# Decoder layer in one core: the FFN weights' own stage taken apart and spread over its neighbours

## What is computed

```python
x = x + attention(layernorm(x), q_w, q_b, k_w, k_b, v_w, v_b, o_w, o_b)   # causal, 16 heads of 32
x = x + long_convolution(ctx, ctx, layernorm(x), ssm_kernel, D)           # kv outer products, convolved, times q
x = x + ffn(layernorm(x), w_gate_up, w_down)

def _quant_dequant(v, axis):
    scale = jnp.max(jnp.abs(v), axis=axis, keepdims=True) / QMAX
    scale = jnp.maximum(scale, EPS)
    q = jnp.clip(jnp.round(v / scale), -QMAX, QMAX)
    return q * scale

gate, up = xq @ w1q.T             # xq: tokens quantised by row; w1q: w_gate_up (2816 x 512), by row
h = silu(gate) * up
out = hq @ w2q.T                  # hq: h quantised by row; w2q: w_down (512 x 1408), by row
```

## Time and profile before

| | |
|---|---|
| median of 3 runs (lowest, highest) | 1241.2 us (1239.53 to 1241.73) |
| the profiled execution, its own time | 1243.32 us |
| its span in the profile | 1241.5 us |
| busy: PE, DVE, POOL, ACT | 1142.1, 1006.6, 963.1, 880.2 us |
| mean granted TensorE clock | 0.965 |
| DMA moved | 186.57 MB, mean 150 GB/s |

### The profile page before, as it was taken

One profiled execution on the slowest core, in us unless ns is written; L12 is line 12 of the kernel. 1 busy time (PEld: TensorE's weight loads), 2 busy tenths in 40 slices (PEclk: granted clock), 3 DMA queues, 4 the chain that ended last, 5 costly groups with the idle time before them and its releaser, 6 DMA issues. The chain is left out here.

```text
span 1241.5 us, 33761 instructions
## 1 busy us (share of the span) xinstructions
PE 1142.1 (92%) x10142; PEld 815.6 (66%) x10142; DVE 1006.6 (81%) x3165; ACT 880.2 (71%) x1815; POOL 963.1 (78%) x1112
## 2 busy tenths in 40 slices
PE   7989999999999999998756799999999999999996
PEld 5767777777777777875435566666666666666652
DVE  4678878878788887887486798888988988988885
ACT  3678888878788887888564366766667666667665
POOL 1286887767777776787833999999999999999993
PEclk8979999999999999999775999999999999999999
DMA  6346755556555555655382444434444333444310
GB/s 206 93 154 193 235 167 171 183 173 190 178 176 171 159 185 166 189 163 182 143 287 70 128 136 142 128 109 131 137 144 140 123 112 129 142 144 132 112 62 26
DMA packets 87840, 186.57 MB, mean 150 GB/s; under 512 B 12176, under 2 KB 28816, under 8 KB 87760
## 3 DMA queue, kind: packets, MB, share of 16 engines
q1 hardware_dynamic: 86896, 185.02, 47.2%
q10 hardware_dynamic: 864, 0.66, 0.3%
HBM read 105.86 MB, written 54.61 MB: 129 GB/s over the span
## 5 line engine op out<-in xcount | busy, mean ns | idle before, releaser
L649 ACT ACTIVATE prob<-masked,negmax 128x128 f32<-128x128 f32 (+1 forms) x512 | 206.4, 454 | 67.6 <-DVE negmax L777 66.6
L777 DVE CUSTOM_DVE_ANT_0 masked<-s_ps,mask_f 128x128 f32<-128x128 f32 (+1 forms) x512 | 161.1, 352 | 34.0 <-PE s_ps L530 21.5
L1028 PE MATMUL y_ps<-kv,toep 128*128 128x288 f16 x640 | 184.2, 288 | 1.4 <-DVE prod L1390 1.4
L1029 PE MATMUL y_ps<-kv,toep 128*128 128x288 f16 x640 | 183.8, 287 | 0.0
L1030 PE MATMUL y_ps<-kv,toep 128*128 128x288 f16 x640 | 183.8, 287 | 0.0
L1086 PE MATMUL f_ps<-w1T,xiT 128*128 128x512 bf16 (+1 forms) x768 | 172.9, 361 | 0.9 <-ACT xiT L1222 0.7
L1286 POOL TENSOR_TENSOR tree<-prod 128x512 f32<-128x512 f32 x128 | 163.3, 1276 | 1.3 <-DVE prod L1390 1.3
L1229 ACT ACTIVATE silu<-gate,sx 128x512 f32<-128x512 f32 (+1 forms) x96 | 66.0, 687 | 134.4 <-DVE gate L1454 134.3
L409 POOL TENSOR_TENSOR kv_s<-kv_f,kv_s 128x1152 f16<-128x1152 f32 x64 | 152.2, 2379 | 0.6 <-ACT kv_s L663 0.6
L783 DVE TENSOR_TENSOR pT_lo<-t_ps,pT_hi 128x384 f16<-128x384 f32 x256 | 140.7, 550 | 12.2 <-ACT pT_hi L657 11.7
L657 ACT CAST pT_hi<-t_ps 128x384 f16<-128x384 f32 x256 | 122.4, 479 | 34.4 <-PE t_ps L539 33.1
(11 more groups left out here) (162 smaller groups left out, 3505.6 us busy)
## 6 DMA issues: line engine op xcount, KB each, us to landing
kv_pairs<-kv_s SPq DMA_DIRECT2D x64, 576.0 KB, 3.3
kv<-kv_pairs SPq DMA_DIRECT2D x32, 1152.0 KB, 8.1
c_in<-in_ctxr SPq DMA_DIRECT2D x64, 192.0 KB, 2.5
x_in<-in_x SPq DMA_DIRECT2D x16, 512.0 KB, 6.4
q_st<-q_hi SPq DMA_DIRECT2D x128, 64.0 KB, 2.0
k_st<-k_hi SPq DMA_DIRECT2D x128, 64.0 KB, 2.0
x_res<-in_x SPq DMA_DIRECT2D x16, 512.0 KB, 5.9
x_after_attention<-x_out SPq DMA_DIRECT2D x16, 512.0 KB, 4.3
```

Of the source, the lines that this page charges most:

```text
L649: ins = nc.scalar.activation(prob[h % 2][:, at:at + w], masked[h % 2][:, at:at + w], ACT.Exp, bias=negmax[:, h % 2, t:t + 1], scale=-1.0)
L777: ins = nc.vector.tensor_tensor_reduce(masked[h % 2][:, at:at + w], s_ps[h % 2][:, at:at + w], mask_f[:, S - w:S], -1.0, FAR, ALU.add, ALU ...
L1028: nc.tensor.matmul(dst, toep[p][:, 0, taps], c[:, 0, m], start=mt == 0, stop=False)
L1029: nc.tensor.matmul(dst, toep[p][:, 0, taps], c[:, 1, m], start=False, stop=False)
```

## The change

The weights stage is gone, and so is its wait of all engines. Its work is spread over three places:

- **Attention's last two rounds**: SP loads all 22 blocks of w_gate_up in 11 loads of 512 KB (`W.load`) and the first convolution's operands (`first_conv`). DVE finds maxima and scales, and ACT scales the rows, for units 0 to 3 between the heads of round 15 and for units 4 to 6 around JOBS_END. The stage no longer waits for `x_stored`.
- **The mixer's beginning**: SP waits for `x_stored` and loads the first tokens and w_down. DVE finds the maxima of units 7 to 10, ACT scales the rows of 7 and 8. PE turns ten half units (four f32 blocks of 128 x 128 each, L194 of the changed kernel) in place, with the rounding constant still on them, then the scales. DVE or ACT takes each set out of PSUM and subtracts the constant on the way.
- **Mixer rounds 0 and 1**: 24 more sets and the scales of w_down, 3 sets at each of five places in round 0 and 2 at each of five in round 1, the maxima of units 11 to 14 and the row scaling of units 9 to 14.

The scales go to HBM and come back as a broadcast DMA (`load_scales`) where before a product with ones spread them. w1T, w2T, q, k, the turned tokens and one convolution buffer now share memory with others. At the program's beginning, the two bias broadcasts are issued later, the key weights are split in two halves, wv is loaded ahead of the second sequence, and `weights_high(2)`, `weights_low(2)`, `row_stats(1)` and `normalise(1)` stand later in their queues.

```diff
+UNITS = [(1, n, 2) for n in range(0, 2 * 11, 2)] + [(2, n, 1) for n in range(DT)]
+N_W1 = 11
+IN_ROUND, IN_TAIL = 4, 7
+UNIT_MAX = {1: 0, 4: 1, 7: 2, 10: 3}
+UNIT_SCALE = {3: 0, 6: 1, 9: 2, 12: 3}
...
+    def home(self, u):
+
+        return self.raw[u // 2][:, u % 2 * 2:u % 2 * 2 + 2, :] if u < 8 else self.x_all[:, 2 * u - 16:2 * u - 14, :]
...
+    def target(self, u, b, nb):
+
+        w, n, _ = UNITS[u]
+        if w == 1:
+            return self.w1T[:, :, (n + b // DT) * P:(n + b // DT + 1) * P]
+        return self.w2T[:, b:b + nb, n * P:(n + 1) * P]
...
+    def find_maxima(self, dve, u):
+        dve.wait_ge(self.loaded[u], 16)
+        rows = self.rows(u)
+        self.nc.vector.tensor_reduce(self.maxima[:, self.columns(u)],
+                                     rows.rearrange("p (k d) -> p k d", d=D) if UNITS[u][0] == 1 else rows, AX_X, ALU.max,
+                                     apply_absolute_value=True).then_inc(self.max_done, 1)
...
+    def scale_rows(self, act, u):
+
+        w, _, k = UNITS[u]
+        rows, inv = self.rows(u), self.inv[:, self.columns(u)]
+        act.wait_ge(self.inv_done, u + 1)
+        for n in range(k):
+            part = rows[:, n * D:(n + 1) * D] if w == 1 else rows
+            ins = self.nc.scalar.activation(part, part, ACT.Copy, bias=MAGIC, scale=inv[:, n:n + 1])
+        ins.then_inc(self.scaled, 1)
...
+    def turn_rows(self, pe, u, b, nb, bank, eye_f):
+        pe.wait_ge(self.scaled, u + 1)
+        rows = self.rows(u)
+        for t in range(nb):
+            mm = self.nc.tensor.transpose(bank[:, t * P:(t + 1) * P], rows[:, (b + t) * P:(b + t + 1) * P], eye_f[:])
+        return mm
...
+        w1T = wqkv[:].rearrange("p a t d -> p (a t d)").bitcast(BF16)[:, 0:DT * 2 * I_FF].rearrange("p (t d) -> p t d", t=DT)
+        w2T = x_all[:].rearrange("p a d -> p (a d)").bitcast(BF16)[:, 0:IT * D].rearrange("p (t d) -> p t d", t=IT)
+        toep_0 = x_all[:, 4 * TT - 1, :].bitcast(F16).rearrange("p (a d) -> p a d", a=2)
+        toep_loaded, kv_loaded = ([top.enter_context(nc.semaphore(f"{n}{p}")) for p in range(2)] for n in ("toep_loaded", "kv_loaded"))
+        W = Weights(nc, top, w1T, w2T, x_all)
...
+    SMALLS = [(bq_raw[:], bq), (bk_s[:], bk), (mask_f[:, S - P:], mask)]
     SMALL = len(SMALLS)
+    BIASES = [(bv_b[:], bv.broadcast_to([P, D])), (bo_b[:], bo.broadcast_to([P, D]))]
+
+    W_PARTS = [[slice(0, D)], [slice(0, D // 2), slice(D // 2, D)], [slice(0, D)], [slice(0, D)]]
+    split_after = lambda n, part=-1: sum(len(W_PARTS[k]) for k in range(n)) + part % len(W_PARTS[n]) + 1
...
+            load_weights(2, wvT)
             load(1)
-            load_weights(2, wvT)
...
+                if isinstance(i, int) and i == B - 2:
+
+                    sp.wait_ge(xn_done, B * TT)
+                    sp.wait_ge(taps_stored, 16)
+                    for half in range(2):
+                        sp.wait_ge(kv_stored[half], 16)
+                    first_conv(sp)
...
+                if last:
+
+                    for j in range(HPT):
+                        sp.wait_ge(stacked[j], (B - 1) * (6 * 16))
+                    W.load(sp, 4, w1)
...
-            sp.wait_ge(w_split, 4)
-            for g in range(2):
-                sp.dma_start(w_raw[g][:], w1[g * DT * P:(g + 1) * DT * P].rearrange("(t p) d -> p t d", p=P)).then_inc(ahead_in, 16)
...
-            sp.wait_ge(x_stored, 16 * B)
-            sp.wait_ge(ahead_in, 32)
+            for u in range(N_W1):
+                sp.wait_ge(W.loaded[u], 16)
...
-            act.wait_ge(eye_in, 16)
             act.wait_ge(small_in, 16 * SMALL)
-            nc.scalar.copy(eye_b[:], eye_f[:])
             nc.scalar.mul(bq_s[:], bq_raw[:], SCALE).then_inc(small_done, 1)
             for k, j in enumerate(JOBS0):
                 high(0, 0, k, j, g_ps[k % G])
                 if k == TT - 1:
                     weights_high(1)
-                if k == TT:
+                    for dst, src in BIASES:
+                        act.dma_start(dst, src).then_inc(bias_in, 16)
+                if k == TT + 1:
                     weights_high(2)
-                if k == TT + 1:
+                if k == TT + DT:
                     normalise(1, TT)
...
+                    if isinstance(i, int) and i == B - 1 and s in UNIT_SCALE:
+                        W.scale_rows(act, UNIT_SCALE[s])
...
+            for u in range(IN_ROUND, IN_TAIL):
+                W.scale_rows(act, u)
...
-                if k == TT:
+                if k == TT + 2:
+                    weights_low(2)
+                if k == TT + DT - 1:
                     row_stats(1)
-                if k == TT + 1:
...
+                    if isinstance(i, int) and i == B - 1 and s - 1 in UNIT_MAX:
+                        W.find_scales(dve, UNIT_MAX[s - 1])
+                    if isinstance(i, int) and i == B - 1 and s in UNIT_MAX:
+                        W.find_maxima(dve, UNIT_MAX[s])
...
+                if k == 2:
+                    for u in range(IN_ROUND, IN_TAIL):
+                        W.find_maxima(dve, u)
+                        W.find_scales(dve, u)
...
+        sp.wait_ge(x_stored, 16 * B)
         load_prep(sp, 0, 0)
-        load_conv(sp, 0, 0)
+        load_down(sp, 0)
         load_prep(sp, 1, 1)
-        load_res(sp, 0)
-
-    ffn_weights(nc, w1, w2, w1T, w2T, s1_b, s2_b, half_neg2, eps2,
...
+    FIRST = HALVES[:10] + ["T"]
+    FIRST_BANK, FIRST_ACT = (0, 1, 2, 3, 4, 5, 0, 1, 2, 3, 0), (0, 1, 3, 5, 7, 9)
+    LATER = HALVES[10:] + DOWNS + ["T2"]
+    STEP_OF = [1 + k // 3 for k in range(15)] + [6 + k // 2 for k in range(10)]
+    BANK_OF = [(0, 1, 6)[k % 3] for k in range(15)] + [k % 2 for k in range(10)]
+    SETS = [(0, item, FIRST_BANK[k], int(k in FIRST_ACT)) for k, item in enumerate(FIRST)]
+    SETS += [(STEP_OF[k], item, BANK_OF[k], int(BANK_OF[k] > 0)) for k, item in enumerate(LATER)]
+    place = lambda k: sum(o[3] == SETS[k][3] for o in SETS[:k])
+    MAX_AT, SCALE_AT = {1: N_W1, 3: N_W1 + 1, 5: N_W1 + 2, 7: N_W1 + 3}, {1: 9, 2: 10, 3: N_W1, 4: N_W1 + 1, 6: N_W1 + 2, 8: N_W1 + 3}
...
+    def load_scales(sp, part):
+
+        rows, n0, n1, out = ((s1_row, 0, 2 * N_W1, s1_b), (s2_row, 2 * N_W1, 2 * N_W1 + DT, s2_b))[part]
+        k = next(k for k, o in enumerate(SETS) if o[1] == ("T", "T2")[part])
+        sp.wait_ge(taken[SETS[k][3]], 1 + place(k))
+        sp.dma_start(sd[n0:n1], rows[:]).then_inc(scales_out, 16)
+        sp.wait_ge(scales_out, 16 * (part + 1))
+        sp.dma_start(out[:], sd[n0:n1].rearrange("n p -> (n p)").unsqueeze(0).broadcast_to([P, (n1 - n0) * P])).then_inc(scales_in[part], 16)
...
+                if isinstance(r, int) and r == 0:
+                    load_scales(sp, 0)
+                    load_res(sp, 0)
...
+            def bank_free(k):
+
+                for n in range(k - 1, -1, -1):
+                    if SETS[n][2] == SETS[k][2]:
+                        pe.wait_ge(taken[SETS[n][3]], place(n) + 1)
+                        return
+
...
+            for k in range(len(FIRST)):
+                turn_set(k)
+                if k == 8:
+                    queries(0)
...
+            take(0)
+            W.scale_rows(act, 7)
+            take(1)
+            W.scale_rows(act, 8)
+            take(3)
+            take(5)
             normalise(0, 0)
+            take(7)
             queries_out(0, 0)
+            take(9)
...
+                nb = item[2]
+                nc.vector.tensor_scalar(W.target(*item), BANKS[bank][:, 0:nb * P].rearrange("p (t c) -> p t c", t=nb), MAGIC, None,
+                                        ALU.subtract).then_inc(taken[0], 1)
...
+            for u in (7, 8):
+                W.find_maxima(dve, u)
+                W.find_scales(dve, u)
             ln_stats(0, 0)
             aggregate(0, st2, st2_done, mv2, mv2_done)
+            take(2)
+            take(4)
+            for u in (9, 10):
+                W.find_maxima(dve, u)
+                W.find_scales(dve, u)
+            take(6)
+            take(8)
+            take(10)
+
+            dve.wait_ge(xq_done, 1)
+            ln_stats(1, 1)
+            aggregate(1, st2, st2_done, mv2, mv2_done)
...
```

380 lines of the change are left out of this document (201 added, 179 removed).

## The result

The changed kernel takes **1227.2 us** (median of 4 runs, 1225.6 to 1229.2), the one before 1241.5 us in the same set (4 runs): a ratio of 0.9886, 95% interval 0.9869 to 0.9902. It is faster by 14.3 us; I had forecast 27.0. The profiled execution took 1225.79 us, 1224.0 of them span.

The account below looks back on a forecast made before the run. DVE bounded the weights stage, POOL's trees mixer rounds 0 and 1. Beginning -5.5, attention +4.0, block start -2.4, start to round 2's first product -24.1, scales +1.0: -27.0 us, median 1241.2 to 1214.2; range 1207 to 1224.

Parts of the forecast that it names:

- three signs of being wrong: Rounds 0 and 1 together over 42 us, attention's last store not before 626, or the loop's rounds differing from before.
- Attention's last rounds: Added units between heads and POOL's later residual cost +4.0 us together; bounds 0 and 11.5; work around JOBS_END nothing.
- The price of a scale: Each DVE scale instruction counted at 0.17 us, two in a unit of 1.22 + 2 x 0.17.
- The beginning: Program's start to head 0's maxima: -5.5 us; -6.1 if PE's clock stays up, -3.4 if it falls.
- The block's start and the opening: Mixer block starts at T = 624.2 (-2.4 us); tokens at T + 5.2, first product at T + 13.1.
- Round 0: Mixer round 0 takes 18 us in place of 10.2 (+7.8); bounds +5 and +15.
- Round 1: Mixer round 1 takes 17.3 us in place of 13.8 (+3.5); bounds +1 and +8.
- The scales' way over HBM: In round 2, SP's store and broadcast of w_down's scales delay head 1's residual: +1.0 us, bounds 0 and +3.
- attention pays more: Rival: all work added to round 15 in series, 11.5 us, and 3.4 gained at the beginning: 1223 to 1224; chance 0.15.
- The clock stays low: Rival: PE's clock low through the opening (+2) and half the work of rounds 0 and 1: 1224 us; chance 0.15.
- The mixer's loop: Rival: loads into shared memory run late in each of 30 rounds; 2 us a round is 1274; chance 0.03.
- the doubt whether the change does what it says: Rival: a w_gate_up load ends after attention and the stage waits, costing as much as it is late; chance under 0.02.

Follow-up runs that it names:

- e11: Changed kernel with the edits of e7 and e9 together; median 1219.9 us, ratio to before 0.9830.
- e9: Changed kernel with each two-column scale (128x2) made by two one-column instructions (128x1) on DVE; median 1226.2 us, ratio 0.9877.
- e2: Changed kernel with weight loads 0 and 1 of round 14 issued behind the pairs' load and store; median 1220.8 us, ratio 0.9853.
- e16: Changed kernel with only the bias broadcasts back in their old place at the front; median 1224.4 us, ratio 0.9872.
- e18: Changed kernel with wk split whole, as before the change, and not in halves; median 1225.0 us, ratio 0.9864.
- e17: Changed kernel with the second sequence's norm and statistics and wv's split back at their old places; median 1226.6 us, ratio 0.9875.
- e7: Changed kernel with only ACT's scaling of units 0 to 3 moved behind the last head; median 1219.4 us, ratio 0.9822.
- e8: Changed kernel with e2's and e3's edits, wv in halves, and PE's wait for all takes behind round 2's first slice; median 1219.9 us, ratio 0.9827.
- e10: Changed kernel with idle PE products (24, 8 and 12) in the opening's waits for takes; median 1226.7 us, ratio 0.9872.
- e15: Changed kernel with the edits of e13 and e14 together; median 1223.6 us, ratio 0.9872.
- e14: Changed kernel with the edits of e2, e7, e9 and e10, wv in halves, and idle PE products in round 1; median 1213.8 us, ratio 0.9795.
- e6: The kernel before the change, run again unedited for a second profile; head 0's maxima at 38.74 us, no median given.
- e13: Changed kernel with e2's, e7's, e9's and e10's edits, wv in halves, and weight loads 2 and 3 moved from round 14 to 15; median 1224.4 us.
- e3: Changed kernel with round 1's turns of step 9, and their take, behind the fourth slice's convolution and product; median 1224.2 us, ratio 0.9881.

## Why the forecast was wrong

I was 9.5 us too low on the profiled pair, and 3.3 more lie between profiles and medians, which the sum could not see. Of my three signs of being wrong one came true, the last store at 626.74 and so not before 626, and it points at the step that failed most. By the forecast's own steps:

- **Attention's last rounds**, forecast +4.0, measured +7.5 (+3.8, +4.2, -0.5): the step that failed most. I counted the units' 11.5 us, took a third of them, and added SP's issues and the last load's bytes for the residual only. Two things were wrong. ACT's scaling stood more than half in series (3.1 of 5.3 us, e11 against e9), although ACT idles 9.1 of 36 us in the earlier trace rows: only two of its gaps there, 2.13 and 1.70 us, are longer than a unit's 1.33. And the loads of round 14, which I counted only against the residual, delayed a store of pairs on which ACT waits (e2: 2.3 us at once, 1.1 to 2.1 by head 15). The median landing of a pairs' store from 540 to 620 us is 3.7 us, of 2.9 before. The wait for the residual, which I did count, grew by 1.5 us and not by 3. The work that I put at nothing around JOBS_END was right: -0.5.
- **The price of a scale**: I took 0.17 us from the earlier trace rows. In round 15 two of four took 2.21 and 1.63 us, 3.5 us of DVE that the sum lacks. Of these at most 0.9 us were on the path in this profile (37.94 against e9's 37.03). The scale of unit 1, short here, was long in six other profiles and cost its full 1.2 to 1.9 us there.
- **The beginning**, forecast -5.5, measured -4.1 by round 14: head 0 comes 4.1 us earlier on average where the clock stays up (34.6), and 2.2 to 2.4 where it falls in V's products. The cause that I gave for it was not the main one. The biases are worth 0.3 us (e16), wk's halves nothing (e18), and the places of the second norm and of wv's split 2 us (e17, one profile, with a wait for the second sequence that the kernel before didn't have). I counted those last two as "no longer held up" without a price. The remaining 1.9 us none of these edits shows alone. In the old order the clock was at 0.52 to 0.62 from 14 to 22 us, after PE's gap of 3.48; that the three edits together keep it up is argued and not shown.
- **The block's start and the opening**, forecast 14.0 from the store, measured 15.3: the first turn came 1.3 us behind the store's issue, not 0.9, and the tokens were there at T+6.3, not T+5.2. Most of that is my estimated landing of 2 us: the tokens came 3.4 us behind their second issue (630.98 and 634.36). From the tokens to the product it took 7.7 us, forecast 7.9.
- **Round 0**, forecast 18 and measured 17.85: right by accident. At full clock it takes 16.0 (e7, e8, e10 to e15), 2 us under what I got from durations at that clock; the rest is the low clock at its beginning.
- **Round 1**, forecast 17.3, measured 20.1: at full clock 18.5. PE's sets and DVE's takes wait for each other (1.4 us at the fourth product), which I had left to the idle; the low clock adds 1.6.
- **The scales' way over HBM**, forecast +1.0, measured 0.0 in round 2, where SP asked for the residual just early enough. The mechanism is real: where the takes come later, it costs 2.25 us as I had described it (e8). In round 1 it delays the tokens of head 2 where round 0 is short (e10, e11, e14, e15: 1.0 to 1.5 us).
- **The end**, forecast 0, measured +1.6. The loop is the same in both; PE's clock fell once behind it, in the windows of 5 us of after, and of before at the same distance from round 3:

```profile
1191.16:1196.16 5.00, 4.84 (x25) 2.71 (x25) 1.78 (x3) 2.39 (x4) 1.20 (x3) 0.66 0.00 0
```
```profile
1210.25:1215.25 5.00, 4.60 (x30) 2.42 (x28) 2.93 (x6) 2.80 (x6) 2.41 (x5) 1.00 0.02 3
```

  The kernel before had the same 2 us more in e6 (528.25 from round 3 to the end), and the changed one ranges from 525.97 (e8) to 530.39 (e10), so nothing shows this to be a part of the change.

Of the rivals, *attention pays more* was the nearest: +7.5 where it had 11.5, and the beginning's 3.4 to 4. *The clock stays low* came true in a part that I did not describe: not through the opening and both rounds, but in two falls of some 4 to 8 us. The Trainium skill, "TensorE: Matmul & The Clock Gate", Part 4 (PE-mode transpose), has it that transposes don't count for the clock; by that rule the opening with turns alone would have stayed at the lower level. The trace disagrees. From 628.04 to 640.40 PE ran nothing but turns, and in windows of after the clock, at its lower level at first, was at its higher one 3 us later:

```profile
628.74:631.24 2.50, 2.50 (x13) 2.50 (x12) 2.31 (x6) 2.14 (x4) 0.00 (x0) 0.50 0.15 47
631.74:634.74 3.00, 1.65 (x15) 1.41 (x13) 0.38 (x1) 1.97 (x4) 0.00 (x0) 1.00 0.85 230
```

The mixer's loop and the doubt whether the change does what it says were rightly small. Three of them at part strength at once (attention, the clock, the beginning) lay outside the range, which I had made of one at a time.

## What to carry to other kernels

Idle time of an engine is room for added work only where its gaps are as long as the work: look for one gap per added instruction, on the engine that the next step of the chain waits for, and else put it behind the last of the chain, as e7 did. A load that is moved into a busy stretch must be checked both ways, for the transfers queued behind it and whose completion holds a buffer (e2), and for when SP really reaches its new place (e13). The same code can have two times, by PE's clock (the opening) or by whether two engines' instructions happen to meet (the scale of unit 1); read a stretch from several profiles before giving it a cause.

## What the runs showed of the hardware

- DVE's tensor_scalar over 128x2 f32 in SBUF waits until POOL's running instruction is done: 0.16 us with POOL idle, 0.4 to 2.3 us beside it and ending with it each time; over 128x1 it takes 0.14 to 0.16 us in any case (e9). POOL's 128x2 tensor_tensor ended with a DVE instruction with two inputs in SBUF and took 1.67 (e17) and 1.90 us (before), of 0.20 otherwise. A DVE scale that began 0.01 us ahead of POOL's was not held (e3's at 582.76).
- PE's granted clock fell or stayed in the same code with the same waits: in the opening, PE's waits of 2.6, 1.0 and 1.4 to 1.5 us ended at 0.50 in the profile of after and at 1.00 in e7's. Idle products in those waits kept it at 1.00 five times out of five. A fall costs round 0 1.8 us in after, 0.3 to 2.0 in the others.
- Turns of f32 alone bring the clock up: 1.74 us for the first eight at S+1.3, 1.04 us for eight from S+5.6 on, the clock at 0.50 from 628.74 to 631.24 and at 1.00 from 631.74.
